# A transformer block on one core: a fourth pair of weight products in the short form, with its mixed weights made by GpSimd in the first block

## The reference, cut to what matters

```
s   = silu(xn @ w_gate.T)                       # 2048 x 2752
s   = s, with the 1376 smallest |s| of each token set to 0
att = (s * (xn @ w_up.T)) @ w_down.T            # 2048 x 1024
h   = relu(xn @ up_w) ** 2                      # 2048 x 2048
moe = ((xn @ fc1_w) @ expert_w.T * (sum of the two largest of xn @ gate_w)) @ fc2_w
y   = x + att + layernorm(h @ down_w + moe) * gamma + beta
```

## Time and profile before

| | |
|---|---|
| median of 3 runs | 2335.4 us (2333.67 to 2336.62) |
| the profiled execution, its own time | 2335.83 us |
| its span, first to last instruction | 2333.7 us |
| TensorE busy | 2317.7 us, 99% of the span |
| VectorE, ScalarE, GpSimd busy | 70%, 47%, 36% |
| DMA | 558.43 MB, mean 239 GB/s |
| TensorE's clock | the upper level in all 40 slices of the page |

### The profile page before, as it was taken

The page is one execution under the profiler, slowest core; times in us unless marked ns, Lnnn a source line. Parts: engine busy times, 40 slices in busy tenths (PEclk is TensorE's granted clock), DMA queues, the critical chain, the costliest instruction groups (busy, mean ns, idle before and its releaser), DMA issues.

```text
span 2333.7 us, 27748 instructions
## 1 busy us (share of the span) xinstructions
PE 2317.7 (99%) x10504; PEld 1927.2 (83%) x10504; DVE 1634.8 (70%) x1810; ACT 1086.9 (47%) x1253; POOL 829.3 (36%) x682
## 2 busy tenths in 40 slices
PE   8999999999999999999999999999999999999999
PEld 6888888888877888888888888888888888888887
DVE  4349999976265989897334598898723568989850
ACT  3247776223233787722124387761213448785110
POOL 5467878796444021123024321304004413030500
PEclk9999999999999999999999999999999999999999
DMA  7798878878898666665778766665667865556555
GB/s 277 280 394 294 292 245 311 293 243 310 287 363 302 206 196 191 204 201 180 234 237 277 249 194 193 195 209 189 207 219 255 279 221 195 193 192 214 180 190 180
DMA packets 191047, 558.43 MB, mean 239 GB/s; under 512 B 20161, under 2 KB 29377, under 8 KB 190913
## 3 DMA queue, kind: packets, MB, share of 16 engines
q1 hardware_dynamic: 190912, 556.65, 71.0%
HBM read 429.62 MB, written 126.94 MB: 238 GB/s over the span
## 4 chain that ended last, share of the span: by engine, by line
PE 93%; DMA 3%; DVE 1%; SPq 1%; POOL 1%; ACT 0%; issue 0%; DVEq 0%; ACTq 0%
PE bank L945 30%; PE bank L947 30%; PE bank L946 30%; PE bank L965 2%; DMA mixed_w<-mixes 1%; DMA split_w<-w 1%; DMA w<-mixed_w 1%; PE bank L956 1%; POOL w L732 0%; SPq L565 0%; SPq L569 0%; PE bank L1038 0%; PE bank L1039 0%; DMA raw<-w_gate_dram 0%; POOL w L735 0%
## 5 line engine op out<-in xcount | busy, mean ns | idle before, releaser
L1292 DVE TENSOR_SCALAR_CACHE_REDUCE junk_v<-mag,cand 128x2816 bf16<-128x2816 f32 x248 | 780.3, 3146 | 8.8
L786 ACT ACTIVATE junk_s<-mag,cand 128x2816 uint8<-128x2816 f32 x248 | 655.4, 2643 | 222.2 <-DVE cand L1284 195.7
L945 PE MATMUL bank<-w,tok 128*128 128x512 f32 (+1 forms) x952 | 365.8, 384 | 1.8 <-DMA w<-split_w 1.7
L947 PE MATMUL bank<-w,tok 128*128 128x512 f32 (+1 forms) x952 | 364.3, 383 | 0.0
L946 PE MATMUL bank<-w,tok 128*128 128x512 f32 (+1 forms) x952 | 364.1, 382 | 0.0
L732 POOL TENSOR_TENSOR w<-raw,w 128x512 fp32r<-128x512 f32 (+1 forms) x196 | 268.1, 1372 | 77.5 <-ACT w L774 67.8
L945 PE MATMUL bank<-w,prod_t 128*128 128x512 f32 x672 | 269.4, 401 | 0.0
L947 PE MATMUL bank<-w,prod_t 128*128 128x512 f32 x672 | 262.8, 391 | 0.0
L946 PE MATMUL bank<-w,prod_t 128*128 128x512 f32 x672 | 261.9, 390 | 0.0
L945 PE MATMUL bank<-tok,w 128*128 128x512 f32 x640 | 249.0, 389 | 0.0
L946 PE MATMUL bank<-tok,w 128*128 128x512 f32 x640 | 249.0, 389 | 0.0
(11 more groups left out here) (149 smaller groups left out, 3728.3 us busy)
## 6 DMA issues: line engine op xcount, KB each, us to landing
w<-split_w SPq DMA_DIRECT2D x516, 512.0 KB, 3.5
split_w<-w SPq DMA_DIRECT2D x192, 512.0 KB, 4.9
w_more<-split_w SPq DMA_DIRECT2D x60, 512.0 KB, 5.2
w<-mixed_w SPq DMA_DIRECT2D x108, 256.0 KB, 3.5
rows<-x_dram SPq DMA_DIRECT2D x32, 512.0 KB, 4.9
raw<-w_down_dram SPq DMA_DIRECT2D x44, 256.0 KB, 3.9
raw<-w_up_dram SPq DMA_DIRECT2D x40, 256.0 KB, 3.1
w<-split_w SPq DMA_DIRECT2D x24, 392.0 KB, 3.5
```

Source lines behind the costliest of these rows:

```text
L786: act.activation(junk_s[:, :, :], mag[:, :, t, :], ACT.Sign, scale=-1.0, bias=cand[:, t:t + 1], accum_out=cnt[:, t:t + 1]).then_inc(counte ...
L945: pe.matmul(out, left[0], right[0], start=first, stop=False)
L947: return pe.matmul(out, left[1], right[0], start=False, stop=last)
L1292: dve.tensor_scalar(junk_v[:, :, :], mag[:, :, t, :], cand[:, t:t + 1], float(1 - (GATED - KEPT)), ALU.is_lt, ALU.add, accum_out=cnt[:, t: ...
```

## The change

The change takes a fourth pair, up 0 and up 1, into the short form in blocks 1 to 3. Those two steps leave the end of the block (they stood right after the shared steps), and 28 short granules follow the third pair. What follows from that in the code:

- The results of the new pair lie in `prod` where the hidden steps put their operands, so they are written to DRAM (`spill`) and loaded again after shared 3 (`load_back`), and their signs are put on in `mask`, one `sign_up` each for groups 0 and 1.
- The operand sums 3 and 4 move from `prod` to `acc`, and are made at granules 10 and 12 of a block, after the last block's stores, not at 2 and 4.
- The search has its first step at granule 101 and its second at 108, within the new pair; the other 29 start at granule 122 and are 11/4 granules apart. It ends at granule 202, and the first of the turned chunks comes after granule 211 (before: 189 and 199).
- The mixed sets 8 to 15, of the third and fourth pair, are made by GpSimd in block 0, from granule 39 on every ten granules (`LATE_SETS`), in `raw_more`, with four loads of 256 KB ahead of each and four stores behind it. VectorE's `mix_later` in block 1 is gone.

```diff
-PAIRS = [(("gate", 0), ("gate", 1)), (("gate", 2), ("gate", 3)), (("gate", GC - 2), ("up", GC - 2))]
-FAST = len(PAIRS)
+PAIRS = [(("gate", 0), ("gate", 1)), (("gate", 2), ("gate", 3)), (("gate", GC - 2), ("up", GC - 2)),
+         (("up", 0), ("up", 1))]
+
+FAST = [0, 4, 4, 4]
 FIRST_PAIRS = 2
+UP_PAIR, SPILLED_PAIR = 2, 3
 PRODUCTS = ["A11 B11", "S2 T2", "A12 B21", "S1 T1", "S4 B22", "S3 T3", "A22 T4"]
-PRODUCT_BANK = [[4, 6, 0, 2, 4, 6, 0], [2, 4, 6, 4, 6, 0, 2], [4, 6, 0, 4, 6, 0, 2]]
+PRODUCT_BANK = [[4, 6, 0, 2, 4, 6, 0], [2, 4, 6, 4, 6, 0, 2], [4, 6, 0, 4, 6, 0, 2],
+                [4, 6, 0, 4, 6, 0, 2]]
...
-        for p in range(FAST if later else FIRST_PAIRS):
+        for p in range(FAST[b] if later else FIRST_PAIRS):
             found += _fast_pair(p) if later else _first_pair(p)
-        steps = _middle + _last
+        steps = [step for step in _middle + _last if step[0] not in sum(PAIRS[:FAST[b]], ())]
...
-            last = end["fast", FAST - 1, len(PRODUCTS) - 1]
-            self.fast_at = {end["fast", p, q] + FAST_LAG: (p, q) for p in range(FAST) for q in range(len(PRODUCTS))
+            last = self.fast_end = end["fast", FAST[b] - 1, len(PRODUCTS) - 1]
+            self.fast_at = {end["fast", p, q] + FAST_LAG: (p, q) for p in range(FAST[b]) for q in range(len(PRODUCTS))
                             if end["fast", p, q] + FAST_LAG < last + 2}
-            self.fast_at.update({last + 2: (FAST - 1, 5), last + 3: (FAST - 1, 6)})
-            self.signs_at = {end["fast", p, q] + FAST_LAG + 3: (p, q) for p in range(FAST - 1) for q in (5, 6)}
-            self.signs_at[last + 4] = (FAST - 1, 6)
-            self.search_from = last + 5
+            self.fast_at.update({last + 2: (FAST[b] - 1, 5), last + 3: (FAST[b] - 1, 6)})
+            self.signs_at = {end["fast", p, q] + FAST_LAG + 3: (p, q) for p in range(UP_PAIR) for q in (5, 6)}
+            up_end = end["fast", UP_PAIR, 6]
+            self.signs_at[last + 4 if up_end == last else up_end + FAST_LAG + 3] = (UP_PAIR, 6)
+        if later and FAST[b] > SPILLED_PAIR:
+            first = up_end + FAST_LAG + 4
+            steps_at = [first, first + 7]
+            steps_at += [last + 3 + (11 * k + 3) // 4 for k in range(BITS + 1 - len(steps_at))]
         else:
-            self.search_from = end[("gate", GC - 2)] + LAG + 1
-        self.search_at = {self.search_from + 3 * k: k for k in range(BITS)}
-        self.search_end = self.search_from + 3 * BITS
+            first = last + 5 if later else end[("gate", GC - 2)] + LAG + 1
+            steps_at = [first + 3 * k for k in range(BITS + 1)]
+        self.search_at = {m: k for k, m in enumerate(steps_at[:BITS])}
+        self.search_from, self.search_end = first, steps_at[BITS]
...
-        self.mask_at = {max(self.search_end + 1 + i, end.get(("up", g), 0) + LAG + 1): g
+        self.back_at = end[("shared", 3)] if FAST[b] > SPILLED_PAIR else None
+        read = {("up", c): self.back_at + 5 + 2 * c for c in range(2)} if self.back_at else {}
+        read.update({key: end[key] + LAG for key in end})
+        self.mask_at = {max(self.search_end + 1 + i, read.get(("up", g), 0) + 1): g
                         for i, g in enumerate(GROUPS[:-1])}
...
-MIX_BLOCK = 1
-MIX_LOADS = {8: range(8, 10), 32: range(10, 11), 40: range(11, 12)}
-MIX_AT = {24: 8, 32: 9, 44: 10, 52: 11}
-MIX_STORES = {26: 8, 34: 9, 46: 10, 54: 11}
+LATE_SETS = {FIRST_MIXES + n: (0, 33 + 10 * n) for n in range(2 * HALF)}
+LATE_LOADS = [{at + i: (n, i) for n, (b, at) in LATE_SETS.items() for i in range(4) if b == c} for c in range(BLOCKS)]
+LATE_AT = [{at + 6: n for n, (b, at) in LATE_SETS.items() if b == c} for c in range(BLOCKS)]
+LATE_STORES = [{at + 8: n for n, (b, at) in LATE_SETS.items() if b == c} for c in range(BLOCKS)]
...
-SUMS_HI_AT = {2: 4, 4: 3}
-SUMS_LO_AT = {2: 4, 4: 3}
+SUMS_HI_AT = [{}, {10: 4, 12: 3}, {10: 4, 12: 3}, {10: 4, 12: 3}]
+SUMS_LO_AT = [{}, {10: 4, 12: 3}, {10: 4, 12: 3}, {10: 4, 12: 3}]
...
-            def load_mix(n):
+            def load_late_mix(n, i):
 
                 p, k = n // HALF, n % HALF
-                if n < FIRST_MIXES + 2:
-                    sp.wait_ge(stored, 16 * (MIX_BLOCK * 2 * TILES + 1))
+                if n == FIRST_MIXES:
+                    sp.wait_ge(mixes_made, 4 * FIRST_MIXES)
                 else:
-                    sp.wait_ge(mixes_stored[n % 2], 16 * (n // 2))
-                for i in range(4):
-                    src, width = words_of((PAIRS[p][i // 2], k + i % 2 * HALF))
-                    sp.dma_start(mix_place(n, i), src).then_inc(mix_loaded[n % 2], 16)
-
-            def store_later_mix(n):
-                sp.wait_ge(later_mixes, 4 * (n - FIRST_MIXES) + 4)
-                words = acc[:, 2 * (n % 2):2 * (n % 2) + 2, :].rearrange("p t (i n) -> p t i n", n=N)
-                sp.dma_start(mixed_w[n].rearrange("(t i) p n -> p t i n", i=2), words).then_inc(mixes_stored[n % 2], 16)
+                    sp.wait_ge(late_stored, 64 * (n - FIRST_MIXES))
+                if n in LATE_AT[1].values():
+                    sp.wait_ge(lo_ready, FIRST_PLAN.count)
+                src, width = words_of((PAIRS[p][i // 2], k + i % 2 * HALF))
+                sp.dma_start(late_place(n, i), src).then_inc(late_loaded, 16)
+
+            def store_late_mix(n, i):
+                sp.wait_ge(late_mixes, 4 * (n - FIRST_MIXES) + 4)
+                sp.dma_start(mixed_w[n, i], late_place(n, i)).then_inc(late_stored, 16)
+
+            def spill(b, c):
+
+                for q in (4, 5) if c else (2, 6):
+                    for j in range(2):
+                        bank, value = emptied(b, ("fast", SPILLED_PAIR, q, j))
+                        sp.wait_ge(bank_emptied[bank], value)
+                sp.dma_start(spilled_u[c], prod[:, 4 * c:4 * c + 4, :, :]).then_inc(spilled[c], 16)
+
+            def load_back(b, c):
+
+                sp.wait_ge(spilled[c], 16 * spills(b))
+                sp.dma_start(prod[:, 4 * c:4 * c + 4, :, :], spilled_u[c]).then_inc(up_back[c], 16)
...
-                if b == MIX_BLOCK:
-                    for n in MIX_LOADS.get(m, ()):
-                        load_mix(n)
-                    if m in MIX_STORES:
-                        store_later_mix(MIX_STORES[m])
+                if m in LATE_LOADS[b]:
+                    load_late_mix(*LATE_LOADS[b][m])
+                if m in LATE_STORES[b]:
+                    for i in range(4):
+                        store_late_mix(LATE_STORES[b][m], i)
+                if plan.back_at:
+                    if m == plan.fast_end + 4:
+                        spill(b, 1)
+                        spill(b, 0)
+                    if m == plan.back_at:
+                        load_back(b, 0)
+                        load_back(b, 1)
...
+            def late_mix(n):
+
+                b11, b21, b12, b22 = (late_place(n, i) for i in range(4))
+                at = 4 * (n - FIRST_MIXES)
+                pool.wait_ge(late_loaded, 64 * (n - FIRST_MIXES + 1))
+                pool.tensor_tensor(b11, b12, b11, ALU.subtract).then_inc(late_mixes, 1)
+                pool.tensor_tensor(b12, b22, b12, ALU.subtract).then_inc(late_mixes, 1)
+                pool.wait_ge(late_mixes, at + 1)
+                pool.tensor_tensor(b22, b22, b11, ALU.subtract).then_inc(late_mixes, 1)
+                pool.wait_ge(late_mixes, at + 3)
+                pool.tensor_tensor(b21, b21, b22, ALU.subtract).then_inc(late_mixes, 1)
...
-                    elif POOL_LO[g] > POOL_LO[g - 1]:
+                    if m in LATE_AT[b]:
+                        late_mix(LATE_AT[b][m])
+                    if b and POOL_LO[g] > POOL_LO[g - 1]:
                         pool.wait_ge(mixed_hi, MIXED[g])
                         pool.tensor_tensor(slot_of(g)[:, 1, :], slot_of(g)[:, 1, :].bitcast(F32), slot_of(g)[:, 0, :],
                                            ALU.subtract).then_inc(pool_lo, 1)
-                    if b and m in SUMS_LO_AT:
+                    if m in SUMS_LO_AT[b]:
                         for j in range(2):
-                            sum_lo(b, SUMS_LO_AT[m], j)
+                            sum_lo(b, SUMS_LO_AT[b][m], j)
...
-                if i > 2:
+                if i > 2 and FAST[b] > SPILLED_PAIR:
+                    act.wait_ge(stored, 16 * (b * 2 * TILES + 1))
+                elif i > 2:
                     act.wait_ge(bank_filled, filled(b - 1, ("out", 1, TILES - 1)))
...
-            def sign_up(b):
-
-                ks = slice(4 * (GC - 2), 4 * (GC - 1))
-                dve.wait_ge(signs_done, b * (GC + 1) + PLANS[b].signs_before[GC - 2] + 1)
-                for j in range(2):
-                    for q in (4, 5):
-                        bank, value = emptied(b, ("fast", FAST - 1, q, j))
-                        dve.wait_ge(bank_emptied[bank], value)
+            def sign_up(b, g):
+
+                ks = slice(4 * g, 4 * g + 4)
+                dve.wait_ge(signs_done, b * (GC + 1) + PLANS[b].signs_before[g] + 1)
```

(13 more changed lines are left out.)

92 lines of the change are left out of this document (50 added, 42 removed).

## The result

| | before | after |
|---|---|---|
| median of 4 runs each | 2334.72 us (2333.67 to 2336.62) | 2393.48 us (2389.57 to 2397.08) |
| ratio, with its 95% interval | | 1.025 (1.0234 to 1.0267) |
| span of the profiled execution | 2333.7 us | 2387.7 us |

The changed kernel is 2.5% slower. The forecast was 1.4%, with a range up to 2390, so the sign was right and the size was not.

The account below looks back on a forecast made before the run. TensorE, busy 2317.7 of 2333.7 us, was taken as the bound. Terms of -16.3 - 5.3 + 33.0 + 8.9 + 4.0 + 1.0 + 7.8 = +33.1 us gave a forecast of 2368.5 us, 1.4% slower, range 2338 to 2390.

Parts of the forecast that it names:

- The matmuls: Blocks 1 to 3: two up steps (43.52 us) give way to a pair (38.08), 16.3 us less in all.
- Block 1's stretch: Block 1's three pairs, without loads and stores of mixed weights, fall from 119.83 to 114.49 us, 5.3 less.
- the operand sums: Two GpSimd operations between low parts of granules 12 and 13 of each block: 1 us in all.
- The first search steps: Search steps now among short granules, ScalarE's counts ahead of granule 104's high parts: no cost, cover 0.6 us or more.
- The clock behind the turned chunks: TensorE at half clock after waits of 9 to 11 us: 2.0 us for each of four waits, granule 40's included.
- The first late set: Block 0, granule 40: TensorE waits 8.9 us for GpSimd's four operations and late loads; bounds 4.2 and 12.
- The end of the search: Blocks 1 to 3: TensorE waits at the first turned chunk for VectorE's reading of up 2, 11.0 us a block.
- The 6.3 us of order: Wait per block from VectorE's queue between reading shared 2 and up 2: bank 0 free at E + 49.8, wanted at E + 43.5.
- I take 8, near the middle: VectorE's waits for ScalarE's counts during the search, 8 us a block (bounds 0 and 14.5), making it 3.7 us late.
- The other seven sets find some lead: Block 0's later sets: 7.6 us spare per ten granules for 5.2 of operations; 4 us lost, bounds 0 and 15.
- Rival D: GpSimd or the DMA bounds all of block 0, later sets cost 15 to 20 us: 2388 to 2410; chance 0.10.
- rival C: Faster: masks before up 2 run unhindered, 11.0 us for 16, wait 0.6 a block: 2321 us; chance 0.15.

Follow-up runs that it names:

- masks_later: Changed kernel with the masks of groups 0 and 1 and their `sign_up` moved behind VectorE's reading of up 2 in blocks 1 to 3: 2356.16 us.
- loads_early: Changed kernel with each late set's four loads issued two by two behind two granules, not one by one behind four: 2383.47 us.
- transfers_only: Changed kernel with the late sets' loads and stores kept but GpSimd's operations on them left out: 2358.94 us.
- half_block1_masks_later: Changed kernel with four late sets in block 1 (three pairs there), others re-placed in block 0, loads two by two, group 0 and 1 masks behind up 2's reading: 2332.32 us.
- spread_no_operations: `half_block1_masks_later` with GpSimd's four operations left out of all eight late sets, waits, loads and stores kept: 2321.18 us.
- no_signs: Changed kernel with the two `sign_up` of groups 0 and 1 left out in blocks 1 to 3, masks kept in place: 2374.20 us.

## Why the prediction was wrong

**What held.** The matmuls: the new pair takes 38.08 us. Block 1's stretch and the operand sums: `masks_later` has block 1 at 563.4, which is 573.6 - 5.4 - 5.3 + 0.5; blocks 2 and 3 likewise leave 0.6 and 0.7 us for the sums, 1.8 in all where 1.0 was taken. They lie in the first pair of each block, beside the sums; each other step took what it took before. The first search steps, spill and load back cost nothing that shows. The clock behind the turned chunks: 2.3 us each by `masks_later`, 2.0 taken. The first late set: granules 37 to 41 lost 10.2 us in all, and 8.9 + 2.0 was forecast for wait and clock.

**The end of the search: right in mechanism, its parts shifted.** The wait was 9.3 us a block on average, 11.0 forecast. The 6.3 us of order stand. "I take 8, near the middle" for ScalarE's waits was too much: in block 1's search they are 2.0 us, so VectorE was 0.3 us late and not 3.7. The 1 us for what GpSimd does beside it was too little: from the first mask to bank 0 the sum was 21.9 us, and it took 24.8. One `sign_up` took 3.37 against 2.28, and the masks of group 1 6.64 for four. The two errors partly cancel, and that the sum came near, 28.0 us measured against 33.0, is in part luck.

**The step that failed** is "The other seven sets find some lead. [...] I take 4 us, bounds 0 and 15." They lost 40.4 - 10.2 = 30.2 us with the clock's share, over 4 a set and twice the upper bound; 2.7 of them are at the wait for VectorE behind the last set. This is all of the miss between the spans, +54.0 measured for +33.1: the other terms, set right, bring the sum down by some 4 us. Three things were left out of it.

- It set 5.2 us of operations against 7.6 us of spare GpSimd time in ten granules, as if GpSimd had only its own work to wait for. I had put in 2 us for a late load at granule 40 and not at the seven others, where GpSimd waited as long (18.0 us in eight). `loads_early` takes that wait away and block 0 gains 7.2 us.
- It counted the DMA as able, 292 and 77 GB/s against 389, and so free. `transfers_only` shows that they cost a lead: 11.3 us fall to 5.4 at granule 59 with no arithmetic at all. Spare was counted twice, once for the transfers and once for the operations, though both draw on one lead; over granules 47 to 116 each costs nothing alone, and together they cost 19.1 us even without the waits for late loads, 27.5 with them.
- It left VectorE out of block 0. With GpSimd's operations beside them VectorE's settlings and hidden low parts take longer, and with the transfers ScalarE's last gate values come later and with them the search. Almost through VectorE alone four well placed sets cost 8.6 us (`half_block1_masks_later` against `spread_no_operations`).

Rival D, with a chance of 0.10, came nearest, and its range (2388 to 2410) holds the measured time. But only half of it is right: it gave the later sets 15 to 20 us where they took 30.2, and made up for that with a delay of VectorE near its upper bound, which was 0.3 us. Against rival C, the masks did not run unhindered: the sixteen ahead of up 2 took 18.7 us, where it had 11.0 and the forecast 16.7.

For the exclusive lock of the Trainium skill ("SBUF — State Buffer", section "SBUF: two separate sides") the bound from it was 2.6 us for the two `sign_up` alone. They lost 1.1 us, within it, and the sixteen masks 2.0; the rule was applied to two instructions where a dozen more stood beside GpSimd's products. That TensorE's clock falls in mid-kernel, as the Trainium skill ("TensorE: Matmul & The Clock Gate", section "Part 1: The HAM clock gate") has it for an idle engine, the windows above show, with PEclk 0.50 behind 9.10 us of wait.

## What to carry to other kernels

Work added to an engine that feeds the bound one must be set against its lead, not against its idle share: write down the lead at the place, subtract every part (its operations, its own wait for their data, the transfers that push its normal loads back), and ask if it is whole again when the next piece comes. If it isn't, every further piece costs what the lead no longer covers, here some 4 us a set. Where a new instruction is short but stands ahead of the reading that frees a bank, its place in the queue matters more than its cost: here moving two masks behind one reading gave back 34.8 us, against 54.0 lost by the change. And look for a stage in which the engine feeds nothing that is waited for: four sets cost 1 us at most beside the plain steps of block 1, whose weights come from DRAM already split.

## What was not expected of the hardware

- VectorE's operations on 128x4 took 0.16 us with GpSimd idle, 0.45 to 0.55 on average beside GpSimd's work in block 0, up to 0.73 with more of it, while its passes over 128x2816 took 3.15 us in every case. The chain of 24 settlings with the sixteen hidden low parts between them grew by 8.4 us. The stretch isn't fixed: after a start 2.1 us later twelve settlings took 1.9 us less in sum.
- TensorE's clock fell at waits of 3.2 to 4.0 us, not only at those of 8 and more; in `no_signs` 1.0 to 1.9 us were lost behind each. In `loads_early` it fell at three waits of 2.4 to 2.6 us, where one of 2.6 in the changed kernel left it at the upper level.
- Transfers and arithmetic of which each alone cost nothing over seventy granules cost 19.1 us together, though GpSimd's idle share and the DMA share of 0.85 before had room for each.
